# A recurrent time-mix and expert kernel: the first step spread over eight PSUM banks and reordered, weights loaded in five groups, and the waits at the start of steps three and seventeen rewritten

## The chip, the cores and the metric

One core of one Trainium2 chip runs the whole program. The metric is the device time of the program in microseconds (us), the median over several executions; lower is better. Before the change it is 1033.22 us (3 runs, 1031.26 to 1033.80).

## What is computed

The input x is (2, 2048, 256), two sequences of 2048 tokens with 256 channels, all in fp32. It is layer-normed, and two branches share the result:

```
xn = layernorm(x)
s = timemix(xn)            # six mixed inputs r,w,k,v,a,g; low-rank tanh products; k normed;
                           # wkv7 recurrence over the tokens, 4 heads of 64; group norm; + bonus; * g; @ oW
g = silu(ffn(xn))          # 8 experts, top 2 of softmax(gate), relu(x wi + bi + lora_e), @ wo
out = x + s * g
```

Inside `timemix`: `dx = x_last - x`, `xm = x + dx*x_miu`, `mix = tanh(xm x_A)`, `miu = lambdas + mix x_B`, and each mixed input is `x + dx*miu` (`xd` in the kernel). Then `k = k_in kW + tanh(k_in k_A) k_B`, divided by its norm; `w` from `tanh(w_in w_A) w_B`; the gates from `a_in a_A a_B` and `tanh(g_in g_A) g_B`; `r` and `v` are full products.

## The kernel before

The 2048 tokens are worked through in 16 tiles of 64 tokens for each of 2 groups and both sequences (`TILES` = 16). The pipeline has three stages, "front" (everything up to r, k, v and the gates of a tile), "rec" (the chunked recurrence and the expert products of the tile before) and "post" (output product and store of the tile before that). So there are `TILES` + 2 = 18 steps; step 1 has front alone, step 2 front and rec, steps 3 to 16 all three, step 17 rec and post, step 18 post.

Each engine has its program written out by hand, one list for each kind of step; engines meet through semaphores alone. `till(name, n)` is the count that a semaphore of the tile in hand must reach. Names that matter below:

- PE (TensorE), from L242: `warm(n)` (L291) issues n products of 256 columns whose result nobody reads. Each product of fp32 stands in the trace as two matmul rows. `xt_`, `route`, `mix`, `miu(0..2)`, `wk_A`, `kW`, `wk_B`, `norm`, `a_A`, `a_B`, `r_`, `xmt_`, `g_A`, `g_B`, `v_` and `bonus_` are the front's products in the order of step 1; with `half=True` a product is split in two of 64 columns of weights that run side by side. `diag` (L439) closes a front. `base`, `lora` (L251) and `gram(l)` (L465) open the recurrence step; `gram(0)` waits in `barrier` (L593) for the end markers of the other three engines, `act_end`, `dve_end` and `pool_end`.
- VectorE: `mixed(k)` (L1393) forms (miu + lambda)*dx into `mtmp`; `first_expert`, `first_mask`, `second_expert`, `expert_masks` and `gate_sum` are chains of very small operations; `key_norm` (L1446, L1447), `kh_` (L1452), `bk0` (L1467), `dg2_` (L1459), `ar1` and `diag_store` end the front.
- GpSimd: `mixed(k)` (L1194) adds xnc to `mtmp` and gives `xd`; `ksum_`, and `bk1` (L1244).
- ScalarE: reads the PSUM banks into SBUF: `hwk` (tanh of wk_A), `kraw_` and `ksq`, `sig_`, `nrm_` (square root), `ha`, `agate_` (sigmoid, of a_B), `r_e`, `xmt_e`, `hg` (tanh of g_A), `ar0`, `gate_`, `v_e`. A change of function can put an `ACT_TABLE_LOAD` in front.
- SP issues the loads. The weights are in four groups, each with one semaphore that counts all its members; PE waits for group 1 before `miu(0)` (L342).

Order and waits in step 1 come from the PSUM banks. `USED_BY` gives every front product bank 3 or 4, the two banks of `miu` too, since in all later steps the recurrence holds the other six. So in step 1 a product waits until the product before it in that bank has been read: `miu(2)` (banks 3 and 4) stands behind `ha_done` and `nrm_done`, `g_A` behind `r_done`, `v_` behind `bonus_done`.

How PE starts a step, L608:

```
full = 4 <= step <= TILES
if step == 2:
    pe.wait_ge(*till("v_done", 0))
    pe.wait_ge(*till("gate_done", 0))
elif not full:
    barrier(step)
```

## Time and profile before

| | us |
|---|---|
| median of 3 runs | 1033.22 |
| the profiled execution | 1030.45 |
| its span (first to last instruction) | 1028.6 |
| step 1: first `gram(0)` of step 2 begins | 47.00 |
| from there to `gram(0)` of step 3 | 62.22 |
| from there to `gram(0)` of step 4 | 62.21 |
| most later steps | 61.35 |

The span is what the trace covers; the profiled execution's own time is 1.85 us longer. In the rows further down, a timeline row reads: start in us, duration in us, engine, line, operation, output and inputs, count, and in brackets how long the engine was idle before and what ended that. PE is the matmul, PEld the weight load. Line numbers are those of the kernel before; in the changed kernel they are 1 to 3 higher.

### The profile page before, as it was taken

How to read it: one execution, taken by the hardware profiler on the slowest of the kernel's cores; microseconds unless marked ns; L12 is line 12 of the kernel's file. 1: busy time of each engine (PE TensorE's matmuls, PEld its weight loads, DVE VectorE, ACT ScalarE, POOL GpSimd, SP SyncE). 2: the span in 40 equal slices, each digit the busy share in tenths (PEclk: the TensorE clock that was granted, in tenths of full speed). 3: DMA queues.
4: the chain of work that ended last, by engine and by line, in shares of the span. 5: the costliest groups of instructions: out<-in, count | busy, mean ns of one | idle time of the engine just before them, and what ended most of it. 6: DMA issues, size and time to landing. Idle time of an engine off the chain costs nothing.

```text
span 1028.6 us, 45507 instructions
## 1 busy us (share of the span) xinstructions
PE 1004.7 (98%) x19960; PEld 787.4 (77%) x19960; DVE 840.2 (82%) x1674; ACT 664.0 (65%) x1460; POOL 457.6 (44%) x541
## 2 busy tenths in 40 slices
PE   8899999999999999999999999999999999999996
PEld 5677777777787777878778787777878778787774
DVE  4597878888898898888888898888889889798764
ACT  3457575766766577675766767577685666757453
POOL 3353353635436353453625436354443725445322
PEclk9999999999999999999999999999999999999998
DMA  7000000000000000000000000000000000000000
GB/s 248 2 13 3 2 4 23 3 23 3 4 23 4 22 3 3 22 4 23 4 23 3 3 23 4 22 4 4 21 4 24 3 23 3 3 22 4 12 4 21
DMA packets 9267, 17.13 MB, mean 17 GB/s; under 512 B 1904, under 2 KB 3824, under 8 KB 8816
## 3 DMA queue, kind: packets, MB, share of 16 engines
q1 hardware_dynamic: 9072, 14.23, 4.3%
q8 instruction: 159, 2.61, 1.1%
q14 instruction: 36, 0.29, 0.1%
HBM read 10.03 MB, written 4.19 MB: 14 GB/s over the span
## 4 chain that ended last, share of the span: by engine, by line
PE 89%; DVE 5%; issue 2%; ACT 2%; SPq 1%; DMA 0%; POOLq 0%; POOL 0%; DVEq 0%
PE bank L251 36%; PE bank L250 13%; PE grams L465 10%; PE bank L342 5%; PE grams L534 2%; PE bank L491 2%; PE bank L480 2%; PE bank L524 2%; PE bank L565 2%; PE grams L589 2%; PE grams L554 2%; PE grams L439 2%; PE bank L357 2%; PE bank L373 2%; PE bank L299 2%
## 5 line engine op out<-in xcount | busy, mean ns | idle before, releaser
L1213 POOL TENSOR_TENSOR bk<-bk,tot 128x256 f32<-128x256 f32 x192 | 154.7, 817 | 214.6 <-PE grams L465 214.6
L1527 DVE COPY_PREDICATED gm<-c_mask_g,grams 128x1024 f32<-128x1024 int32 x96 | 160.2, 1669 | 15.1 <-PE grams L465 14.4
L899 ACT ACTIVATE relu<-bank,prm 128x256 f32<-128x256 f32 x256 | 107.3, 471 | 88.0 <-PE bank L251 86.7
L1194 POOL TENSOR_TENSOR xd<-mtmp,xnc 128x512 f32<-128x512 f32 x96 | 120.9, 1274 | 35.9 <-DVE mtmp L1393 35.9
L251 PE MATMUL bank<-xnc,w_wi 128*128 128x256 f32 x512 | 125.5, 388 | 3.8 <-ACT scratch L1181 2.1
L465 PEld LDWEIGHTS grams<-ar,bk 64*64 64x64 f32 x6144 | 100.9, 135 | 23.2 <-issue 15.4
L1003 ACT ACTIVATE gl<-gm 32x128 f32<-32x128 f32 x320 | 98.9, 309 | 28.6 <-DVE gm L1527 21.9
L251 PE MATMUL bank<-xmt,w_lora_B 128*128 128x256 f32 x444 | 114.5, 387 | 0.0
L465 PE MATMUL grams<-ar,bk 64*64 64x64 f32 x6144 | 112.0, 221 | 2.4 <-ACT scratch L1181 2.3
L251 PEld LDWEIGHTS bank<-xnc,w_wi 128*128 128x128 f32 x512 | 95.0, 191 | 22.2 <-issue 6.9
L1537 DVE TENSOR_TENSOR ar<-ar,tot 128x512 f32<-128x512 f32 x96 | 93.1, 970 | 20.9 <-PE grams L465 20.9
L1393 DVE SCALAR_TENSOR_TENSOR mtmp<-bank,prm,dx 128x256 f32<-128x256 f32 x192 | 80.3, 473 | 29.0 <-PE bank L342 29.0
L1244 POOL TENSOR_TENSOR bk<-kh,rootd 128x512 f32<-128x512 f32 x16 | 28.2, 1763 | 151.9 <-PE bank L524 150.3
L251 PEld LDWEIGHTS bank<-xmt,w_lora_B 128*128 128x128 f32 x444 | 80.5, 190 | 15.1 <-issue 5.0
L250 PE MATMUL bank<-w_wo,hid 128*64 128x256 f32 x768 | 90.9, 379 | 0.0
L250 PEld LDWEIGHTS bank<-w_wo,hid 128*64 128x64 f32 x768 | 52.6, 137 | 23.3
L342 PE MATMUL bank<-mixt,w_x_B 32*128 32x256 f32 x384 | 54.4, 400 | 1.1 <-DMA c_headsel<-c_headsel_dram 0.9
L1225 POOL TENSOR_TENSOR out_t<-out_t,x_in 128x512 f32<-128x512 f32 x16 | 20.3, 1270 | 76.7 <-DVE out_t L1516 76.7
L1495 DVE TENSOR_TENSOR hid<-relu 128x512 f32<-128x512 f32 x64 | 48.3, 775 | 0.6
L910 ACT ACTIVATE xnc<-bank 128x512 f32<-128x512 f32 x16 | 9.6, 598 | 50.8 <-PE bank L299 50.8
L945 ACT ACT_TABLE_LOAD x32 | 41.1, 1283 | 0.6
L1576 DVE TENSOR_TENSOR state<-dec,bank 128x256 f32<-128x256 f32 x32 | 13.4, 418 | 33.2 <-PE bank L575 33.2
(189 smaller groups left out, 2232.6 us busy)
## 6 DMA issues: line engine op xcount, KB each, us to landing
x_in<-x SPq DMA_DIRECT2D x16, 256.0 KB, 2.7
out<-out_t SPq DMA_DIRECT2D x16, 256.0 KB, 2.0
w_wi<-w_wi_dram SPq DMA_DIRECT2D x1, 1024.0 KB, 6.3
w_wo<-w_wo_dram SPq DMA_DIRECT2D x1, 1024.0 KB, 8.6
w_lora_B<-w_lora_B_dram SPq DMA_DIRECT2D x1, 512.0 KB, 7.3
w_x_A<-w_x_A_dram SPq DMA_DIRECT2D x1, 256.0 KB, 2.7
w_x_B<-w_x_B_dram SPq DMA_DIRECT2D x1, 256.0 KB, 2.8
w_kW<-w_kW_dram SPq DMA_DIRECT2D x1, 256.0 KB, 3.3
```

The lines of the kernel that those rows point to most:

```text
L250: last = mm(out[o:o + 64, :], lhsT[:, o:o + 64], rhs, **kw)
L251: return last if half else mm(out, lhsT, rhs, **kw)
L342: last = mm(MIU[k % 2][:, c * 256:(c + 1) * 256], w["x_B"][o:o + 32, u, c * 128:(c + 1) * 128], mixt[o:o + 32, u, :], start=True, stop=True)
L465: last = mm(dst, bk[o:o + 64, g, c, 1 - b, k, :], rhs, start=True, stop=True)
L899: A(dst[:, p % 2, j * 256:(j + 1) * 256], ZB[p % 2][:, j * 256:(j + 1) * 256], ACT.Relu, bias=prm[:, P_BI + 2 * p + j:P_BI + 2 * p + j + 1 ...
L1003: A(gl[l % 2][o:o + 32, :, :, :].rearrange("p q g (c n m) -> p (q g c) n m", c=2, m=m), right(gm[o:o + 32, :, :, :, b, 0, 32 * k:32 * k + ...
L1194: tt(xd[:, q, :, :], mtmp[:, k % 2, :, :], xnc[steps["front"] % 2][:, :, :], ALU.add).then_inc(S(f"xd_{k}_done"), 1)
L1213: tt(v, v, d, ALU.mult).then_inc(S(f"bk{k}_scaled"), 1)
L1393: run(v.scalar_tensor_tensor(mtmp[:, k % 2, c, :], MIU[k % 2][:, c * 256:(c + 1) * 256], prm[:, P_LAM + 2 * q + c:P_LAM + 2 * q + c + 1], ...
L1495: run(v.tensor_tensor(hid[:, p, :], relu1[:, p % 2, :], relu2[:, p % 2, :], ALU.add), f"hid_{p}_done")
L1527: run(v.copy_predicated(dst, msk.to_broadcast([128, 32, HALF // m, m]), src), "g_stored")
L1537: run(v.tensor_tensor(a, a, tv[:, :, 0].unsqueeze(1).unsqueeze(3).to_broadcast([128, 2, 4 * n, m]), ALU.mult), "ar_scaled")
```

## The change

In step 1 a table of its own, `FIRST_USED_BY`, spreads the front's products over banks 0 to 6, and `warm` writes bank 7 in place of 2. With it go a new order on PE, ScalarE, VectorE and GpSimd in step 1, other numbers of `warm` products, and a weight group more. At the start of steps the waits of PE are rewritten. The diff, cut to its core:

```diff
+FIRST_USED_BY = {"xt": 0, "route": 2, "mix": 1, "kW": 5, "wk_A": 6, "g_A": 0, "wk_B": 2, "a_A": 1, "a_B": 5, "norm":
+           6, "r": 0, "v": 2, "g_B": 1, "xmt": 5, "bonus": 6}
...
-            return bank[USED_BY[name]]
+            return bank[(FIRST_USED_BY if steps["front"] == 0 else USED_BY)[name]]
...
-        SECOND = ["x_B", "w_A", "k_A", "a_A", "wk_B", "a_B", "kW", "rW", "vW", "g_A", "g_B", "ones", "headsel"]
+        SECOND = ["x_B", "w_A", "k_A", "wk_B", "kW"]
-        THIRD = ["wi", "lora_B"]
+        THIRD = ["ones", "a_A", "a_B", "g_A", "rW", "vW", "g_B", "headsel"]
+        FOURTH = ["wi", "lora_B"]
...
-                    mm(CB[:, 0:256], xnc[1][:, 0, 0:128], xnc[1][:, 1, :], start=True, stop=True)
+                    mm(FB[:, 0:256], xnc[1][:, 0, 0:128], xnc[1][:, 1, :], start=True, stop=True)
...
-                full = 4 <= step <= TILES
+                full = 3 <= step <= TILES
                 if step == 2:
-                    pe.wait_ge(*till("v_done", 0))
-                    pe.wait_ge(*till("gate_done", 0))
-                elif not full:
+                    pe.wait_ge(*till("mx_4_done", 0))
+                    pe.wait_ge(*till("mx_5_done", 0))
+                    pe.wait_ge(*till("xmt_done", 0))
+                    pe.wait_ge(*till("bonus_done", 0))
+                elif step == TILES + 2:
                     barrier(step)
                 if step == 1:
-                    warm(6)
+                    warm(5)
...
+                        warm(4)
                         if step == 1:
                             wait_loaded(pe, 1)
                         miu(0)
-                        warm(3)
+                        warm(4)
...
                         miu(1)
+                        kW(half=True)
+                        wk_A()
+                        wait_loaded(pe, 2)
+                        g_A(half=True)
+                        wk_B()
+                        a_A()
+                        miu(2)
+                        a_B()
+                        norm()
+                        warm(2)
+                        r_()
+                        v_()
+                        g_B()
                         xmt_()
+                        warm(3)
+                        bonus_()
                         pe.wait_ge(*till("r_done", 1))
+                        pe.wait_ge(*till("gate_done", 1))
                         diag(rec)
...
                         hwk()
+                        hg()
                         kraw_()
+                        ha()
                         sig_()
+                        agate_()
                         nrm_()
-                        ha()
-                        agate_()
                         r_e()
+                        gate_(step)
+                        ar0(rec)
                         xmt_e()
-                        hg()
-                        ar0(rec)
-                        gate_(step)
                         v_e(rec)
...
                         mixed(1)
                         mixed(0)
+                        mixed(3)
+                        mixed(2)
                         ksum_()
-                        mixed(2)
-                        mixed(3)
...
-                        first_mask()
-                        second_expert()
                         mixed(1)
                         mixed(0)
                         mixed(3)
                         mixed(2)
+                        gate_sum()
+                        first_mask()
+                        second_expert()
                         expert_masks()
                         mixed(4)
+                        mixed(5)
                         decay_step(rec)
-                        mixed(5)
                         key_norm()
                         kh_()
+                        dg2_()
                         bk0(rec)
-                        dg2_()
+                        ar1(rec)
                         bonus_e(rec)
-                        gate_sum()
-                        ar1(rec)
...
                         top_x()
+                        pe.wait_ge(*till("v_done", 0))
                         keys_to_tokens(0)
...
                         rec_p(1)
+                        pe.wait_ge(*till("gate_done", 0))
                         keys_to_tokens(1)
```

The last two pieces are step 17's; in step 17's own list `barrier(step)` still stands as the first entry, ahead of `gram(0)`, in both kernels. `full` also puts the waits for `v_done` before `xt_` and for `gate_done` before `route` in step 3.

PE in the middle of step 1, before: `a_A` (a_A), `miu(2)` (x_B), `a_B`, `r_` (rW), with `warm` products (xnc) between.

```order
L363 MATMUL bank<-xd,w_a_A 64x256 [waits xd_2_done,sig_done]
L363 MATMUL bank<-xd,w_a_A 64x256
L294 MATMUL bank<-xnc 128x256 x4
L342 MATMUL bank<-mixt,w_x_B 128x256 [waits mixt_done,ha_done,nrm_done]
L342 MATMUL bank<-mixt,w_x_B 128x256 x3
L294 MATMUL bank<-xnc 128x256 x2
L251 MATMUL bank<-h_a,w_a_B 128x256 [waits ha_done,mx_4_done]
L251 MATMUL bank<-h_a,w_a_B 128x256
L251 MATMUL bank<-xd,w_rW 128x256 [waits xd_4_done,mx_5_done]
L251 MATMUL bank<-xd,w_rW 128x256 x3
```

The same place in the changed kernel, from `a_A` on:

```order
L366 MATMUL grams<-xd,w_a_A 64x256 [waits xd_2_done,mixt_done]
L366 MATMUL grams<-xd,w_a_A 64x256
L345 MATMUL bank<-mixt,w_x_B 128x256 [waits mixt_done,mx_3_done,mx_2_done]
L345 MATMUL bank<-mixt,w_x_B 128x256 x3
L254 MATMUL bank<-h_a,w_a_B 128x256 [waits ha_done,ksq_done,kraw_done]
L254 MATMUL bank<-h_a,w_a_B 128x256
L254 MATMUL bank<-ksum,c_ones 128x256 [waits ksum_done,hwk_done]
L297 MATMUL bank<-xnc 128x256 x2
L254 MATMUL grams<-xd,w_rW 128x256 [waits xd_4_done,hg_done]
L254 MATMUL grams<-xd,w_rW 128x256 x3
```

`miu(2)` follows `a_A` directly and no longer waits for `ha_done` and `nrm_done`; `norm` (ksum) has moved behind `a_B`.

PE at the end of step 1, before: `bonus_` (dg), `g_B`, `v_` (vW), `diag` (rr), and the first product of step 2 (wi).

```order
L446 MATMUL bank<-dg,c_headsel 32x128 [waits dg2_done,xmt_done]
L446 MATMUL bank<-dg,c_headsel 32x128 x3
L251 MATMUL bank<-w_g_B,h_g 128x256 [waits hg_done]
L251 MATMUL bank<-w_g_B,h_g 128x256
L251 MATMUL bank<-w_vW,xd 128x256 [waits xd_5_done,bonus_done]
L251 MATMUL bank<-w_vW,xd 128x256 x3
L439 MATMUL grams<-rr,bk 64x64 [waits r_done,bk1_ready,bk0_ready]
L439 MATMUL grams<-rr,bk 64x64 x31
L251 MATMUL bank<-xnc,w_wi 128x256 [waits v_done,gate_done,big_buffers_zeroed,xnc_done,weights_loaded_3,weights_loaded_2]
```

The same place in the changed kernel; the `warm` products stand ahead of `bonus_`:

```order
L297 MATMUL bank<-xnc 128x256 x3
L449 MATMUL bank<-dg,c_headsel 32x128 [waits dg2_done,nrm_done]
L449 MATMUL bank<-dg,c_headsel 32x128 x3
L442 MATMUL grams<-rr,bk 64x64 [waits bk1_ready,bk0_ready,r_done,gate_done]
L442 MATMUL grams<-rr,bk 64x64 x31
L254 MATMUL bank<-xnc,w_wi 128x256 [waits mx_5_done,mx_4_done,xmt_done,big_buffers_zeroed,bonus_done,weights_loaded_4,xnc_done,weights_loaded_3,weights_loaded_2]
```

`g_B` and `v_` have gone from between `bonus_` and `diag`, and step 2 no longer waits for `v_done`.

PE at the start of step 3, before: `v_`, `base(1)` (wi), `lora(1)`, `gram(0)`.

```order
L251 MATMUL bank<-w_vW,xd 128x256 [waits xd_5_done,bonus_done]
L251 MATMUL bank<-w_vW,xd 128x256 x3
L251 MATMUL bank<-xnc,w_wi 128x256 [waits xnc_done,dve_end,relu2_3_done,pool_end,act_end]
L251 MATMUL bank<-xnc,w_wi 128x256 x3
L251 MATMUL bank<-xmt,w_lora_B 128x256 [waits xmt_done]
L251 MATMUL bank<-xmt,w_lora_B 128x256
L465 MATMUL grams<-ar,bk 64x64 [waits dve_end,pool_end,act_end]
```

The same place in the changed kernel:

```order
L254 MATMUL bank<-w_vW,xd 128x256 [waits xd_5_done,bonus_done]
L254 MATMUL bank<-w_vW,xd 128x256 x3
L254 MATMUL bank<-xnc,w_wi 128x256 [waits relu2_3_done,xnc_done]
L254 MATMUL bank<-xnc,w_wi 128x256 x3
L254 MATMUL bank<-xmt,w_lora_B 128x256 [waits xmt_done]
L254 MATMUL bank<-xmt,w_lora_B 128x256
L468 MATMUL grams<-ar,bk 64x64 [waits dve_end,pool_end,act_end]
```

The three end markers have gone from `base(1)` and stand ahead of `gram(0)` alone.

## Rows read from the trace of the kernel before

**Rows 1.** The page: busy time by engine, the chain that ended last.

```profile
PE 1004.7 (98%) x19960; PEld 787.4 (77%) x19960; DVE 840.2 (82%) x1674; ACT 664.0 (65%) x1460; POOL 457.6 (44%) x541
...
PE 89%; DVE 5%; issue 2%; ACT 2%; SPq 1%; DMA 0%; POOLq 0%; POOL 0%; DVEq 0%
```

**Rows 2.** Stretches of step 1 (us; PE, PEld, DVE, ACT, POOL busy; PEclk; DMA share; GB/s).

```profile
37.28:40.70 3.42, 3.42 (x15) 2.52 (x13) 1.59 (x6) 0.60 (x1) 0.00 (x0) 0.50 0.00 0
33.87:37.28 3.41, 1.52 (x12) 0.86 (x13) 2.60 (x4) 1.86 (x4) 1.87 (x2) 1.00 0.01 2
```

**Rows 3.** DMA issues (KB, us to landing), then start, us, engine of SP and PE.

```profile
w_kW<-w_kW_dram SPq DMA_DIRECT2D x1, 256.0 KB, 3.3
...
7.35 0.43 SPq L1799 DMA_DIRECT2D w_kW<-w_kW_dram  x1
...
11.89 0.59 PE L294 MATMUL bank<-xnc 128*128 128x256 f32 x2
13.36 1.13 PE L342 MATMUL bank<-mixt,w_x_B 32*128 32x256 f32 x8 [0.87 <-DMA c_headsel<-c_headsel_dram]
```

**Rows 4.** Timeline of step 1, first half: DVE, GpSimd and PE.

```profile
14.54 1.66 DVE L1393 SCALAR_TENSOR_TENSOR mtmp<-bank,prm,dx 128x256 f32<-128x256 f32 x4 [2.10 <-PE bank L342]
...
15.49 2.49 POOL L1194 TENSOR_TENSOR xd<-mtmp,xnc 128x512 f32<-128x512 f32 x2 [11.08 <-DVE mtmp L1393]
...
16.25 1.13 PE L342 MATMUL bank<-mixt,w_x_B 32*128 32x256 f32 x8 [0.27 <-DVE mtmp L1393]
```

**Rows 5.** Timeline of ScalarE, 22 to 32 us.

```profile
23.37 1.28 ACT L945 ACT_TABLE_LOAD   x1
...
26.82 0.38 ACT L977 ACTIVATE nrm<-bank 128x256 f32<-128x256 f32 x1
...
27.62 0.38 ACT L931 ACTIVATE h_a<-bank 128x256 f32<-128x256 f32 x1
```

**Rows 6.** Timeline of VectorE and GpSimd, 29 to 38 us, and one line's durations.

```profile
29.26 0.88 DVE L1393 SCALAR_TENSOR_TENSOR mtmp<-bank,prm,dx 128x256 f32<-128x256 f32 x2 [9.29 <-PE bank L342]
...
31.17 0.58 DVE L1446 TENSOR_SCALAR nrm<-nrm 128x256 f32<-128x256 f32 x1
...
33.64 0.69 DVE L1452 TENSOR_TENSOR kh<-kraw,kinv 128x512 f32<-128x512 f32 x1
...
36.15 0.87 DVE L1459 SCALAR_TENSOR_TENSOR dg<-rr,prm,kh 128x256 f32<-128x256 f32 x2
...
34.41 1.27 POOL L1244 TENSOR_TENSOR bk<-kh,rootd 128x512 f32<-128x512 f32 x1 [1.54 <-DVE kh L1452]
...
L1467 DVE SCALAR_TENSOR_TENSOR bk<-kh,agate x16: 691/692/1347, 34.9 to 955.8; 128x512 f32<-128x512 f32 x16
```

**Rows 7.** Timeline of PE, end of step 1 and start of step 2.

```profile
39.56 2.46 PE L251 MATMUL bank<-w_vW,xd 128*128 128x256 f32 x8
41.95 1.16 PE L439 MATMUL grams<-rr,bk 64*64 64x64 f32 x64
44.24 1.97 PE L251 MATMUL bank<-xnc,w_wi 128*128 128x256 f32 x8 [1.14 <-ACT vt L973]
...
47.00 1.17 PE L465 MATMUL grams<-ar,bk 64*64 64x64 f32 x64
```

**Rows 8.** The same at step 2 to 3, with ScalarE's end marker.

```profile
102.46 1.89 PE L251 MATMUL bank<-w_vW,xd 128*128 128x256 f32 x8
106.46 1.97 PE L251 MATMUL bank<-xnc,w_wi 128*128 128x256 f32 x8 [2.11 <-ACT scratch L1181]
...
109.22 1.17 PE L465 MATMUL grams<-ar,bk 64*64 64x64 f32 x64
```

**Rows 9.** The same at step 3 to 4, and at step 16 to 17.

```profile
167.02 1.89 PE L251 MATMUL bank<-w_vW,xd 128*128 128x256 f32 x8
...
171.43 1.17 PE L465 MATMUL grams<-ar,bk 64*64 64x64 f32 x64
...
968.91 1.85 PE L465 MATMUL grams<-ar,bk 64*64 64x64 f32 x64 [2.32 <-ACT scratch L1181]
```

More of the change, by code:

```diff
@@ L96, in program @@
         x_first = ctx.enter_context(nc.semaphore("first_x_loaded"))
-        loaded_by = [ctx.enter_context(nc.semaphore(f"weights_loaded_{i}")) for i in range(4)]
+        loaded_by = [ctx.enter_context(nc.semaphore(f"weights_loaded_{i}")) for i in range(5)]
         zeroed = ctx.enter_context(nc.semaphore("buffers_zeroed"))
@@ L628, in tile @@
                         miu(1)
-                        warm(1)
-                        pe.wait_ge(*till("mx_3_done", 2))
-                        wk_A()
-                        pe.wait_ge(*till("mx_2_done", 2))
-                        kW(half=True)
-                        pe.wait_ge(*till("hwk_done", 1))
-                        wk_B()
-                        warm(4)
+                        kW(half=True)
+                        wk_A()
+                        wait_loaded(pe, 2)
+                        pe.wait_ge(*till("xnc_done", 1))
@@ L637, in tile @@
+                        g_A(half=True)
+                        pe.wait_ge(*till("route_read", 1))
+                        wk_B()
+                        pe.wait_ge(*till("mixt_done", 2))
+                        a_A()
+                        pe.wait_ge(*till("mx_2_done", 2))
+                        pe.wait_ge(*till("mx_3_done", 2))
+                        miu(2)
                         pe.wait_ge(*till("kraw_done", 1))
                         pe.wait_ge(*till("ksq_done", 1))
-                        norm(half=True)
@@ L640, in tile @@
-                        warm(1)
+                        a_B()
+                        pe.wait_ge(*till("hwk_done", 1))
+                        norm()
+                        warm(2)
+                        pe.wait_ge(*till("hg_done", 1))
+                        r_()
                         pe.wait_ge(*till("sig_done", 2))
-                        a_A()
-                        warm(4)
-                        pe.wait_ge(*till("nrm_done", 1))
+                        v_()
                         pe.wait_ge(*till("ha_done", 1))
-                        miu(2)
@@ L647, in tile @@
-                        warm(2)
-                        pe.wait_ge(*till("mx_4_done", 2))
-                        a_B()
-                        pe.wait_ge(*till("mx_5_done", 2))
-                        r_()
+                        g_B()
                         pe.wait_ge(*till("agate_done", 2))
                         xmt_()
+                        warm(3)
+                        pe.wait_ge(*till("nrm_done", 1))
+                        bonus_()
                         pe.wait_ge(*till("r_done", 1))
-                        g_A()
@@ L656, in tile @@
-                        pe.wait_ge(*till("xmt_done", 1))
-                        bonus_()
-                        pe.wait_ge(*till("hg_done", 1))
-                        g_B()
-                        pe.wait_ge(*till("bonus_done", 1))
-                        v_()
+                        pe.wait_ge(*till("gate_done", 1))
                         diag(rec)
@@ L881, in tile @@
                     wait_loaded(pe, 3)
+                    wait_loaded(pe, 4)
                     pe.wait_ge(zeroed_late, len(ZEROED_LATE))
@@ L1774, in tile @@
                         if step == 1:
[L1775 removed]
+                            wait_loaded(dve, 4)
                             dve.wait_ge(zeroed_late, len(ZEROED_LATE))
@@ L1809, in _ @@
                     load(3)
+                    load(4)
                 if step >= 3:
```

17 lines of the change are left out of this document (5 added, 12 removed).

## Prediction

> **What bounds the kernel now.** I read the page first. PE is busy for 98% of the span and carries 89% of the chain that ended last [rows 1], so in general only PE's own work and the places where PE has nothing to do are worth anything. The change leaves the steady steps alone: PE's order in steps 2 to 18 is the same, only waits differ. So I looked at two places: step 1, where there is no recurrence to fill PE, and the seams between steps. The stretches of step 1 show what is left there: from 33.87 to 37.28 us PE is busy for 1.52 of 3.41 us, and in the next 3.42 us it is busy throughout but at a granted clock of 0.50, that is 1.2 GHz [rows 2]. Then the timelines of each engine, in the order in which the wait ends last: loads, VectorE, ScalarE, VectorE again, PE.
>
> **Step 1, up to miu(0).** Before, miu(0) is released at 13.36 us by headsel, the thirteenth load of its group [rows 3]. The group of five ends with w_kW, which even at its old place (issued at 7.35, 3.3 us to landing) is there at 10.65 us [rows 3]. So that wait is gone. But three more warm products stand in its place. The warm products after mix begin at 11.89 us [rows 3]. Ten products of this shape (v_, base, lora) take 167.02 to 171.43, 0.44 us each [rows 9], so four last until 13.65 us. miu(0) begins 0.3 us **later** than before: the new group gains nothing here. miu(1) follows 2.89 us behind it [rows 3, 4], the four warm products between (1.76 us, after 1.1 us of miu) fit in just that, and mtmp and xd on VectorE and GpSimd keep their distance [rows 4]. miu(1) is at 16.55 us, and GpSimd's first two xd end at 18.3.
>
> **Up to ksq.** PE now does kW, wk_A and g_A where it did one warm product, wk_A and kW. By 0.44 a product that is some 0.9 for g_A less 0.44 and less a wait for mtmp: wk_B comes about 0.2 us later than before, and so do kraw and ksq, whose end before is the table load at 23.37 [rows 5]. Now 23.6 us.
>
> **ScalarE to nrm.** Before, 23.37 to 26.82 holds a table load (1.28), the sigmoids, and another load: 3.45 us, so 0.89 for a pair of sigmoids [rows 5]. The new order adds h_a (0.38 alone, some 0.3 in a row of reads) before and the pair of agate within: 23.6 + 0.3 + 3.45 + 0.85 = 28.2, and nrm (0.38) ends at 28.55, which is 1.35 us later than its 27.20 of before [rows 5]. That agate's product is there in time rests on miu(2) and a_B: miu(2) starts at about 22.9, a_B follows h_a at about 24, agate is not due until 26.
>
> The Trainium skill, page ScalarE: Activation LUTs, section What ACT_TABLE_LOAD costs, puts a switch at about 1.28 us of load and 1.38 us of drain, 2.66 in all. By that the two switches of this chain would cost 2.8 us more, and the time would be 1025.0. The trace has 1.28 and nothing beside it at these two.
>
> **VectorE to kh.** Here is the first gain. Before, VectorE sat idle for 9.29 us until 29.26 because miu(2) stood behind ha_done and nrm_done, and key_norm began only at 31.17 although nrm was there at 27.20 [rows 5, 6]. Now miu(2) is done at 24.0, mixed(4) and mixed(5) (0.88 each [rows 6]) fit before 26.5, and key_norm begins with nrm at 28.6. From key_norm to the end of kh is 31.17 to 34.33, 3.16 us [rows 6], of which some 0.1 or 0.2 was the first operation being held up. kh ends at 31.6: **2.73 us earlier**.
>
> What hides the rest: the chains of small operations (first_mask and so on) now run between mixed(2) and mixed(4), 19.5 to about 24.5; each 1 us more pushes r_ back by 1. The PE chain r_ (from 26.7), v_, g_B, xmt, warm(3) is about 14 products or 6.2 us and ends at 32.9, 0.9 ahead of its due time. If that cover is gone, every us over it counts.
>
> **kh to diag.** Before: bk0, dg2, then bonus, g_B and v_ on PE, the last two at the half clock (v_ takes 2.46 against 1.89 [rows 7, 8]), then diag at 41.95: 7.62 us after kh [rows 6, 7]. Now g_B and v_ lie ahead, and dg2 (0.87) and bk0 remain. GpSimd's bk1 starts with the same signal and takes 1.27 [rows 6]. bk0 took 1.35 beside it and 0.69 in the median [rows 6], so a VectorE operation is held while GpSimd runs. Between "not held" (0.87 + 0.69, diag at 33.3) and "held to the end of bk1" (1.27 + 0.87 + 0.69, diag at 34.5) I take the second, because the row of step 1 is the very case. That is 2.9 us after kh in place of 7.62: **4.72 us earlier**.
>
> **diag to gram(0) of step 2.** Before 5.05 us, with 1.14 of waiting for the last copy of v [rows 7]. Now base(1) waits for xmt_done and bonus_done instead. bonus_e ends at about 35.4, diag's 1.1 us of issue at 35.6, so they just fit. Then 44.24 to 47.00, 2.76 us [rows 7]: gram(0) comes 3.85 us behind diag, at 38.35. **1.20 us earlier**. The end markers don't hold it: diag_store (1.3 us) ends 2.6 us behind diag, the copies of v on ScalarE at about 35.2. If ScalarE were 2.8 us later than that, it would be the end.
>
> Together 2.73 + 4.72 + 1.20 = **8.65 us**. The order of functions on ScalarE also ends step 1 with the square root, and the load ahead of step 2's std goes; base(0) and lora(0) cover that time on PE, so nothing is counted (0 to 0.3).
>
> **Step 3.** Before, PE idles 2.11 us for act_end, then base(1); v_ to gram(0) is 102.46 to 109.22, 6.76 us [rows 8]. At the next seam, where base and lora already stand ahead of the wait, it is 4.41 [rows 9]. Difference **2.35 us**. The idle time of before ended with act_end at 106.46 [rows 8], so a gram(0) at 102.46 + 4.41 = 106.87 is not early for it. The added waits for v_done and gate_done come after gram(0), which has waited for act_end, and cost nothing.
>
> **Step 17.** The barrier is taken from the head of the step, but the step's own list still begins with it ahead of gram(0), so the idle 2.32 us [rows 9] stay: 0. If it worked as the words of the change say, PE could have saved those 2.3 (1019.9); the order of the changed kernel excludes that.
>
> **Sum.** 8.65 + 2.35 = 11.0 us. Against the profiled execution 1030.45 - 11.0 = 1019.45; the median of the runs lies 2.77 above that execution, so 1033.22 - 11.0 = **1022.2**.
>
> **Rivals.**
> - *VectorE isn't held by bk1.* 1.2 us more, 1021.0. For it: dg2 could start before GpSimd takes its turn. Chance 0.12.
> - *The clock falls at the end of step 1.* Before it fell after 33.87 to 37.28, with PE busy for 1.52 us [rows 2]. Now PE is thin from 33 to 34.5 alone. A stretch of 3.4 us at 1.2 GHz costs up to 1.7: 1023.9. Chance 0.12.
> - *The barrier at step 3 only changes places*: gram(0) is held by the markers. Then 2.35 is lost, 1024.55. Against it stands the seam behind it. Chance 0.04.
> - *The table switch has its drain* in the new order: 1025.0. Chance 0.04.
> - *Slower: the clock is never granted in step 1.* One warm product fewer stands at the start, and PE has a gap ahead of xt_. The new step 1 has some 52 products of 0.44, 23 us; at 1.2 GHz that is some 20 more, of which 4 fall into gaps: 1022.2 + 16 = 1038. It decides from 11 us of such work on. Before, the granted clock was 1.00 from 33.87 to 37.28 [rows 2], with a start that differs by one product of six, so 0.01. The Trainium skill, page TensorE: Matmul & The Clock Gate, section What's actually happening, says that the default is throttled and activity releases it; by that rule too one product fewer matters little.
>
> **How the numbers follow.** The forecast has 0.62, the rivals 0.33, and 0.05 is left for what I don't see. The range: a gain of 8.5 us (clock and some small delays, 1024.7) to 13 (not held, the saved table load, fewer stalls of issue, which are 2% of the chain [rows 1]; 1020.2), and 0.5 to 1 for the scatter of the median, whose three runs lie 2.5 apart: 1019.2 to 1025.2. About 0.3% (3.1 us) is what a measurement of this kernel can tell from no change. Faster by more 0.96, within it 0.02, slower 0.02.
>
> **What would show it.** Right: miu(0) at about 13.6, not earlier; miu(2) at 23 and VectorE's long idle gone; kh at 31 to 32; diag within 3 us of kh; PEclk 1.00 up to 969 us; gram(0) of step 2 at 38, of step 3 some 59.9 later; the seam at step 17 unchanged. Wrong: PE idle ahead of bonus_ or diag for over 1.5 us, VectorE's small operations running past 25, PEclk at 0.50 after 30, or a start of step 3 still behind ACT scratch.

## The result, and the profile after

The changed kernel takes **1017.13 us** (median of 4 runs, 1016.44 to 1018.04) against 1032.24 us for the kernel before beside it (4 runs, 1030.65 to 1033.80): a ratio of 0.9862, with a 95% interval of 0.9842 to 0.9881. Two later sets gave 0.9869 [0.9846, 0.9892] and 0.9867 [0.9852, 0.9882]. These four runs of the kernel before lie high: the medians differ by 15.1 us here, by 13.5 and 13.6 in the later sets, which have 13 runs of it each. I take 13.7 us as the gain; the narrowest of the intervals allows 12.2 to 15.2. The forecast was 1022.2, in a range from 1019.2 to 1025.2. The direction was right, the time lies below the range.

| | before | after |
|---|---|---|
| the profiled execution, us | 1030.45 | 1017.24 |
| its span | 1028.6 | 1015.4 |
| `gram(0)` of step 2 begins | 47.00 | 38.25 |
| from there to `gram(0)` of step 3 | 62.22 | 59.56 |
| `gram(0)` of step 17 begins | 968.91 | 956.80 |

The page of the changed kernel, beside [rows 1]. PE's busy time is 6.8 us less, with eight matmul rows fewer: the kernel hardly computes less, it waits less and computes less slowly.

```profile
span 1015.4 us, 45487 instructions
...
PE 997.9 (98%) x19952; PEld 783.6 (77%) x19952; DVE 842.5 (83%) x1674; ACT 660.5 (65%) x1458; POOL 457.3 (45%) x541
...
PE 93%; DVE 3%; issue 2%; ACT 2%; POOLq 0%; POOL 0%; DVEq 0%
```

**Step 1.** PE's timeline in the changed kernel, which answers to [rows 3, 4, 7]:

```profile
12.01 1.89 PE L297 MATMUL bank<-xnc 128*128 128x256 f32 x8
13.83 1.13 PE L345 MATMUL bank<-mixt,w_x_B 32*128 32x256 f32 x8
...
23.09 1.13 PE L345 MATMUL bank<-mixt,w_x_B 32*128 32x256 f32 x8
...
33.68 0.43 PE L449 MATMUL bank<-dg,c_headsel 128*32 128x128 f32 x8 [0.30 <-DVE dg L1460]
34.34 1.16 PE L442 MATMUL grams<-rr,bk 64*64 64x64 f32 x64 [0.24 <-issue]
35.49 1.97 PE L254 MATMUL bank<-xnc,w_wi 128*128 128x256 f32 x8
...
38.25 1.17 PE L468 MATMUL grams<-ar,bk 64*64 64x64 f32 x64
```

`miu(0)` begins with the end of the warm products, not with a load. `miu(2)` is at 23.09, where before it was held until 28.09 by the reads of two banks. `diag` is at 34.34 in place of 41.95, and behind it there is no wait any more.

VectorE in the same stretch, beside [rows 6], and then ScalarE, beside [rows 5]:

```profile
24.73 1.65 DVE L1394 SCALAR_TENSOR_TENSOR mtmp<-bank,prm,dx 128x256 f32<-128x256 f32 x4
...
28.61 0.29 DVE L1447 TENSOR_SCALAR nrm<-nrm 128x256 f32<-128x256 f32 x1 [1.39 <-ACT nrm L978]
28.94 1.75 DVE L1448 RECIPROCAL kinv<-nrm 128x256 f32<-128x256 f32 x1
30.81 0.69 DVE L1453 TENSOR_TENSOR kh<-kraw,kinv 128x512 f32<-128x512 f32 x1
31.61 1.92 DVE L1460 SCALAR_TENSOR_TENSOR dg<-rr,prm,kh 128x256 f32<-128x256 f32 x2
33.45 0.68 DVE L1468 SCALAR_TENSOR_TENSOR bk<-kh,agate 128x512 f32<-128x512 f32 x1
```

```profile
24.03 1.28 ACT L946 ACT_TABLE_LOAD   x1
25.32 0.84 ACT L946 ACTIVATE sig<-bank,prm 128x256 f32<-128x256 f32 x2
26.05 0.84 ACT L946 ACTIVATE agate<-bank,prm 128x256 f32<-128x256 f32 x2
26.90 1.28 ACT L978 ACT_TABLE_LOAD   x1
28.20 0.38 ACT L978 ACTIVATE nrm<-bank 128x256 f32<-128x256 f32 x1
```

The idle time of 9.29 us on VectorE is gone, and the longest wait left in this stretch is 1.39 us for nrm. The pair of dg takes 1.92 us beside GpSimd's bk1.

**The seams.** Step 2 to 3, where the wait of 2.11 us of [rows 8] is gone:

```profile
93.40 1.89 PE L254 MATMUL bank<-w_vW,xd 128*128 128x256 f32 x8
95.13 1.89 PE L254 MATMUL bank<-xnc,w_wi 128*128 128x256 f32 x8
96.86 1.03 PE L254 MATMUL bank<-xmt,w_lora_B 128*128 128x256 f32 x4
97.81 1.17 PE L468 MATMUL grams<-ar,bk 64*64 64x64 f32 x64
```

and step 16 to 17, where most of it stayed, beside [rows 9]:

```profile
956.80 1.17 PE L468 MATMUL grams<-ar,bk 64*64 64x64 f32 x64 [2.01 <-ACT scratch L1182]
```

What differs here is less the wait (2.01 for 2.32) than the matmuls: 1.17 us for 64 of them, against 1.85 in the kernel before. Its own stretches tell why (columns: PE, PEld, DVE, ACT, POOL busy; PEclk; DMA share; GB/s; kernel before):

```profile
965.70:969.12 3.42, 1.10 (x18) 0.68 (x20) 2.68 (x6) 2.08 (x5) 0.19 (x1) 1.00 0.10 37
969.12:972.53 3.41, 3.41 (x68) 2.97 (x62) 1.72 (x1) 0.00 (x0) 1.67 (x3) 0.50 0.00 0
```

and the same place and the end of step 1 in the changed kernel, there with PE alone:

```profile
33.86:37.28 3.42, 3.18 (x80) 1.00 0.03 5
...
950.00:953.40 3.40, 3.40 (x85) 1.00 0.02 5
953.40:957.00 3.60, 1.59 (x19) 1.00 0.20 73
```

Before, PE ran at 1.2 GHz for 3.4 us behind the seam at step 17, with work in all of it. After, the granted clock stays 1.00 there and at the end of step 1 ([rows 2] have 0.50 from 37.28 on).

**Where 13.2 us between the two profiled spans lie**, read as distances on PE between `mix`, `miu(0)`, `diag` and `gram(0)` of the two timelines:

| stretch | before | after | gain |
|---|---|---|---|
| start to `mix` | 10.11 | 10.28 | -0.17 |
| `mix` to `miu(0)`, step 1 | 3.25 | 3.55 | -0.30 |
| `miu(0)` to `diag`, step 1 | 28.59 | 20.51 | 8.08 |
| `diag` to `gram(0)` of step 2 | 5.06 | 3.91 | 1.15 |
| `gram(0)` to `diag`, step 2 | 53.40 | 53.09 | 0.31 |
| `diag` to `gram(0)` of step 3 | 8.82 | 6.47 | 2.35 |
| `gram(0)` to `diag`, step 3 | 55.74 | 55.43 | 0.31 |
| `diag` to `gram(0)` of step 17 | 6.27 | 5.96 | 0.31 |
| `gram(0)` of step 17 to the end | 59.70 | 58.60 | 1.10 |

Together 13.1; the steps between them give the other 0.1. The row "`gram(0)` to `diag`, step 3" is no part of the change: over all profiled executions, with and without the change, it lies between 54.8 and 56.5, by stalls of issue that come and go.

Two of these rows hide something that only further executions show. From `miu(0)` to `diag` the old step 1 takes 26.94 or 26.95 us in each of the five profiled executions that have it with the granted clock at 1.00 (two of them with more warm products), and the new one 20.51 or 20.52 in eight. So the change itself is worth 6.44 us there, and the other 1.64 of the 8.08 is the stretch at 1.2 GHz of the first profiled execution. And `miu(0)` of before waits for a load, which in that execution landed early. In the kernel before, profiled again (c_before_a), the same row reads:

```profile
13.90 1.13 PE L342 MATMUL bank<-mixt,w_x_B 32*128 32x256 f32 x8 [1.84 <-DMA c_headsel<-c_headsel_dram]
```

From `mix` to `miu(0)` it is 3.25, 4.22, 3.69, 4.05 and 4.08 us in the five executions with the loads and the one warm product of before, 3.86 in the mean, and 3.55 in every one with the new loads and four warm products.

### The profile page after: what moved, and what is told of

It reads as the page before. It is cut to its first block, busy times and chain, and to the rows that moved or that the text cites. A ratio compares the mean times of both kernels' runs of the same rounds, so it can differ in the third digit from the quotient of the medians.

```text
span 1015.4 us, 45487 instructions
## 1 busy us (share of the span) xinstructions
PE 997.9 (98%) x19952; PEld 783.6 (77%) x19952; DVE 842.5 (83%) x1674; ACT 660.5 (65%) x1458; POOL 457.3 (45%) x541
## 4 chain that ended last, share of the span: by engine, by line
PE 93%; DVE 3%; issue 2%; ACT 2%; POOLq 0%; POOL 0%; DVEq 0%
PE bank L254 37%; PE bank L253 14%; PE grams L468 10%; PE bank L345 5%; PE bank L494 2%; PE grams L537 2%; PE bank L483 2%; PE bank L527 2%; PE grams L442 2%; PE bank L568 2%; PE grams L592 2%; PE grams L557 2%; PE bank L360 2%; PE bank L376 2%; PE bank L302 2%
## 5 line engine op out<-in xcount | busy, mean ns | idle before, releaser
L254 PEld LDWEIGHTS bank<-xmt,w_lora_B 128*128 128x128 f32 x444 | 80.5, 190 | 15.1 <-issue 5.0
L1203 POOL TENSOR_TENSOR tot<-tot 128x256 f32<-128x256 f32 (+2 forms) x96 | 39.5, 412 | 2.7
```

What stands on the lines that cost most here:

```text
L254: return last if half else mm(out, lhsT, rhs, **kw)
```

## The experiments

**The halves.** First the two kernels unchanged, beside everything else.

c_before_a (the kernel before): 

> The kernel before, unchanged, for its own scatter. Theory A (the runs of before that lie above its fastest are executions in which the clock fell at a seam where PE had nothing to do): times from 1030 to 1034, and the slower ones have the lower mean granted clock, about 0.990 at 1033.5 against 0.993 at 1030.5. Rival B (the scatter has nothing to do with the clock): the same spread with the same mean clock in all.

Measured 1030.98 (10 runs, 1029.21 to 1033.76), ratio 1.0001 [0.9988, 1.0015]. In step 1 its profiled execution had the slow stretch at another place than the first: a granted clock of 0.50 from 15.48 on for 6.8 us, where the first had it at 37.28; at step 17 both had one. The slower runs have the lower clock, as theory A has it: 0.990 in the one of 1033.76 us, 0.995 in the one of 1029.21.

c_after (the changed kernel): 

> The changed kernel, unchanged, beside the kernel before on the same chip. Theory A (part of the gain is clock falls that no longer come): about 14 us less than the median of before (1031), that is 1017, with a spread of about 1.5 and a mean granted clock of 0.995 or more. Rival B (my prediction's way of counting, the gap between median and profiled execution stays the same in both kernels): the same 11 us less, 1020.

Measured 1017.22 (4 runs, 1015.71 to 1017.81), ratio 0.9869.

e_first_only: step 1 and step 2 as changed, the waits of steps 3 and 17 as before.

```diff
-                full = 3 <= step <= TILES
+                full = 4 <= step <= TILES
...
-                elif step == TILES + 2:
+                elif not full:
                     barrier(step)
```

> The changed kernel with the old starts of steps 3 and 17 (barrier at their head). The first step's part alone. By the traces: gram(0) of step 2 at 38.25 in place of 47.00 (8.75) and 0.3 in step 2 (no table load ahead of std): about 9.0 us less than before. Theory A: 1023 with the same scatter of about 3 as before, since the idle seam 2 to 3 is still there. Rival B: 1023 as well; rival C (the two parts help each other beyond their sum): over 1024.

Measured 1022.01 (4 runs), ratio 0.9913 [0.9886, 0.9939]: 9.0 us of the gain. A and B said the same here, so it decides only against C.

e_seams_only: the kernel before, with the changed waits of steps 3 and 17 alone.

```diff
-                full = 4 <= step <= TILES
+                full = 3 <= step <= TILES
...
-                elif not full:
+                elif step == TILES + 2:
                     barrier(step)
...
+                        pe.wait_ge(*till("v_done", 0))
                         keys_to_tokens(0)
...
+                        pe.wait_ge(*till("gate_done", 0))
                         keys_to_tokens(1)
```

> The kernel before with the new starts of steps 3 and 17 alone. By the traces 2.35 us at step 3; at step 17 the same three markers are waited for once in place of twice, which my prediction priced at nothing and the trace of the changed kernel shows as 0.3 us (2.01 idle in place of 2.32). Theory A: 2.65 and another 1 to 1.5 of clock falls that no longer come at step 3: about 1028.4. Rival B: 2.65 alone, 1029.6; rival D (the 0.3 at step 17 is chance): idle 2.3 at step 17, 1029.9.

Measured 1027.46 (9 runs), ratio 0.9969 [0.9957, 0.9981]: 3.2 us. The timelines give the seams 2.35 + 0.31 = 2.66, with 6.47 and 5.96 us from `diag` to `gram(0)`, as in the changed kernel. That rules out rival D; A (3.65 to 4.15) and B (2.65) both lie within the interval of 2.0 to 4.4 us. The halves add up to 12.2 of 13.7, within the intervals. In e_first_only the seams' idle time is still there, and PE's timeline shows what it costs beside itself:

```profile
96.87 2.82 PE L254 MATMUL bank<-xnc,w_wi 128*128 128x256 f32 x8 [2.12 <-ACT scratch L1182]
99.48 1.90 PE L254 MATMUL bank<-xmt,w_lora_B 128*128 128x256 f32 x4
101.32 1.17 PE L468 MATMUL grams<-ar,bk 64*64 64x64 f32 x64
```

The eight rows take 2.82 us, where the changed kernel has 1.89, and the four 1.90 in place of 1.03. The seam is 10.52 us long in this execution: 8.82 and 1.7 more of slow clock.

**The terms of the sum, one by one.**

e_warm1: one warm product ahead of `miu(0)` in place of four.

```diff
                         mix()
-                        warm(4)
+                        warm(1)
```

> The changed kernel with one warm product in place of four ahead of miu(0), the number that the kernel before has there. Theory (miu(0) stands behind these products and nothing else, mixt being there at 12.85): miu(0) at 12.9 in place of 13.83, everything up to diag 0.9 earlier, 1016.2. Rival (the chain to diag starts later than miu(0), or the products hold the clock up): diag at 34.3 as now or later, 1017 or more, with a fall of the clock in the record.

PE's timeline of e_warm1:

```profile
11.46 0.59 PE L297 MATMUL bank<-xnc 128*128 128x256 f32 x2
12.45 1.13 PE L345 MATMUL bank<-mixt,w_x_B 32*128 32x256 f32 x8 [0.39 <-ACT mixt L920]
```

`miu(0)` stands 1.0 us behind the warm product's start in place of 1.82, and `mix` to `diag` is 23.23 in place of 24.07: 0.84 us, all of which the chain passes on. The median is 1016.65 (4 runs), ratio 0.9866. That is less than 0.84 below the changed kernel, and the two intervals overlap, so the traces show this gain and the medians don't resolve it. What `miu(0)` waits for now is ScalarE's second piece of mixt, by 0.39 us.

e_group: the changed kernel with the weight groups of before. 

```diff
-        SECOND = ["x_B", "w_A", "k_A", "wk_B", "kW"]
+        SECOND = ["x_B", "w_A", "k_A", "a_A", "wk_B", "a_B", "kW", "rW", "vW", "g_A", "g_B", "ones", "headsel"]
...
-                        wait_loaded(pe, 2)
                         pe.wait_ge(*till("xnc_done", 1))
```

> The changed kernel with the weights in the four groups of before (headsel thirteenth in the second group). Theory A (the new group gains nothing, since miu(0) stands behind the four warm products): miu(0) at 13.6 to 13.9 and gram(0) of step 2 at 37.8 to 38.3, as in the changed kernel. Theory B (the group matters): miu(0) later than 14.2 and everything behind it by as much.

```profile
11.79 1.89 PE L297 MATMUL bank<-xnc 128*128 128x256 f32 x8
13.85 1.13 PE L345 MATMUL bank<-mixt,w_x_B 32*128 32x256 f32 x8 [0.17 <-DMA c_headsel<-c_headsel_dram]
```

`miu(0)` at 13.85 against 13.83, but `mix` began earlier here: from `mix` to `miu(0)` it is 3.78 for 3.55, and `mix` to `diag` is 24.30, 0.2 more. The one run took 1018.20 us. In this execution the load ends just behind the warm products, and the fifth group is worth 0.2 us. In the seven executions with the old loads and the old step 1, `miu(0)` was released between 13.36 and 14.13, and in most executions of the changed kernel the warm products are done by 13.4, so elsewhere the group should be worth up to some 0.7 us, an estimate from these rows. It is also what e_warm1 needs, with `miu(0)` at 12.45.

e_bk1_dve: GpSimd's bk1 of step 1 moved to VectorE, behind bk0.

```diff
                         bk0(rec)
+                        bk1_v()
...
-                        bk1(rec)
```

> The changed kernel with bk1 of step 1 on VectorE, behind bk0, instead of on GpSimd. Theory A (dg2 of VectorE was held by GpSimd's bk1 for 1.05 us): dg2 takes 0.87 each, bk0 ends 1.0 earlier, bk1 then costs 0.7 to 0.9 on VectorE but diag needs only dg2 and bk0, or bk1 too: diag 0.2 to 1.0 us earlier, mix to diag 23.1 to 23.9 against 24.07. Theory B (dg2 was slow for a reason of its own): dg2 stays at 1.92 and diag comes 0.7 to 0.9 us later.

VectorE's timeline of e_bk1_dve:

```profile
31.17 0.88 DVE L1459 SCALAR_TENSOR_TENSOR dg<-rr,prm,kh 128x256 f32<-128x256 f32 x2
31.97 0.68 DVE L1467 SCALAR_TENSOR_TENSOR bk<-kh,agate 128x512 f32<-128x512 f32 x1
32.57 0.68 DVE L1474 TENSOR_TENSOR bk<-kh,rootd 128x512 f32<-128x512 f32 x1
```

The pair of dg takes 0.88 when GpSimd is idle and 1.92 when it is not: the hold is real, and it was GpSimd's. `mix` to `diag` is 23.66, 0.41 less, since bk1 now takes 0.6 of VectorE's own time. The median, 1017.65 (4 runs), shows nothing of it; the profiled execution lost more at step 17, where its clock fell.

e_vwait: the two waits of before put back at the head of step 2.

```diff
                     pe.wait_ge(*till("bonus_done", 0))
+                    pe.wait_ge(*till("v_done", 0))
+                    pe.wait_ge(*till("gate_done", 0))
```

> The changed kernel with the two waits of before (v_done, gate_done) put back at the head of step 2, beside the new ones. Theory A (v is read out of its bank before diag's last product is issued): diag to gram(0) 3.9 to 4.2 us. Theory B (the move of the two waits is what the seam gains): 4.4 us or more.

`diag` to `gram(0)` is 4.01 for 3.91, and the one run took 1016.29. All other executions with the new step 1 have 3.91. So the seam of step 2 gained by v being early, not by the waits being other ones; two waits that are already met cost 0.10.

e_sqrt_end: the kernel before with a square root in ScalarE's order behind `ar0`, so that step 1 ends with that table.

```diff
                         ar0(rec)
+                        A(scratch[:, 0:1], eps[:, 0:1], ACT.Sqrt)
                         gate_(step)
```

> The kernel before with one square root of a scratch column on ScalarE near the end of step 1, where ScalarE is idle, so that step 2 finds the table of the square root in place. Theory: this is the whole of the 0.3 us that step 2 is shorter in the changed kernel: from gram(0) of step 2 to that of step 3 61.9 in place of 62.22 (clock falls aside), gram(0) of step 2 where it was. Rival: 62.2 as before, and the 0.3 comes from VectorE's later start in step 2. The median 0.3 less, which the timing can't tell; the trace decides.

ScalarE's load ahead of rstd in step 2 (47.97 in the kernel before) is gone, and `gram(0)` to `diag` of step 2 is 53.11 in place of 53.40, just the 53.09 of the changed kernel. The load lay on the path with at most 0.3 of its 1.28 us: e_fill, e_fill2 and e_fill3 below keep it and have 53.26, 53.25 and 53.26, with nothing changed in step 2, so half of the difference may be something else. The median is 1030.85, ratio 1.0004 [0.9990, 1.0018]: too small for it.

e_base17: step 17 as its description has it, with `base(1)` and `lora(1)` ahead of the barrier.

```diff
+                        base(1)
+                        lora(1)
                         barrier(step)
                         gram(0)
-                        base(1)
-                        lora(1)
```

> The changed kernel with what the words of the change say of step 17: base(1) and lora(1) ahead of the barrier, then gram(0) and gram(1). The rival of my prediction prices this at 2.0 us less (the idle time of PE). Other theory: step 17 hangs on VectorE's chain gram(0), store, scale, gram(1), so what counts is when gram(0) begins; base and lora end 0.6 us after the markers, so gram(0) is 0.6 later and the time 0.6 more, though PE's idle time at the seam is gone.

Measured 1018.31 (4 runs), ratio 0.9881 [0.9863, 0.9898], not faster than the changed kernel. PE has work until `gram(0)`, but that now begins 4.41 us behind `v_`, where the changed kernel has 3.90, and the chain on VectorE behind it comes later by as much, with less of PE's work left to cover it:

```profile
956.47 1.17 PE L468 MATMUL grams<-ar,bk 64*64 64x64 f32 x64
957.70 2.47 DVE L1528 COPY_PREDICATED gm<-c_mask_g,grams 128x1024 f32<-128x1024 int32 x1 [1.67 <-PE grams L468]
959.99 0.87 DVE L1538 TENSOR_TENSOR ar<-ar,tot 128x512 f32<-128x512 f32 x1
960.91 1.39 PE L468 MATMUL grams<-ar,bk 64*64 64x64 f32 x44 [3.28 <-DVE ar L1538]
```

PE idles 3.28 us for `ar` instead of 2.01 for the marker and 0.50 for `ar`, and its stretches show the clock that follows:

```profile
957.60:961.04 3.44, 0.16 (x11) 0.13 (x11) 3.16 (x2) 0.79 (x3) 3.19 (x5) 1.00 0.00 0
961.04:964.45 3.41, 3.41 (x68) 3.02 (x69) 1.56 (x2) 0.45 (x2) 2.18 (x5) 0.50 0.02 5
```

So the forecast was right that the change does not do this, and wrong that it would have saved 2.3 us: `gram(0)` begins 0.5 us later behind `v_`, and the time is no shorter.

**What the terms leave over.** The timelines' terms without slow clock are worth about 10.9 us (worked out in the next section), the measured gain is some 13.7, so 2.8 are left, 1.3 to 4.3 by the interval. Theory A: the rest is time at 1.2 GHz that the kernel before pays behind its idle seams. Rival B: waits that the timelines don't show.

e_fill: the kernel before, with products that nobody reads in the idle time of the seams; nothing is taken away.

```diff
                 elif not full:
+                    if step in (3, TILES + 1):
+                        warm(4)
                     barrier(step)
```

> The kernel before with four warm products ahead of the barrier in steps 3 and 17, so that PE is busy for 1.7 of its 2.1 to 2.3 idle us there. No work is taken out. Theory A: the granted clock no longer falls after these two seams; the median goes down by 1 to 2 us to about 1030.5 and its spread to under 2; in the profile the interval from v_ to gram(0) of step 3 stays at 6.76. Rival B: median and spread as before, 1032.2 and 3.

Measured 1029.11 (10 runs), ratio 0.9987 [0.9971, 1.0003]. In its profiled execution the granted clock falls behind neither seam, as A has it, but its runs spread over 4.0 us where A said under 2, and the interval reaches 1: leaning to A, open.

e_fill2: meant as e_fill with more products in step 1, but its four products of steps 3 and 17 stand behind the barrier, so the idle time is not filled as the expectation has it.

```diff
                     barrier(step)
...
+                if step in (3, TILES + 1):
+                    warm(4)
```

> The kernel before with more work and none taken away: four warm products at the head of steps 3 and 17, one more ahead of miu(0), three ahead of bonus_ and two behind diag in step 1, all where PE idles. Theory A (the part of the gain that the timelines don't explain, 2.8 us, is time at 1.2 GHz that the kernel before pays in most executions and the changed one does not): granted clock 1.00 up to the tail, median 1027.5 to 1029, and a scatter no wider than that of the changed kernel (2 us). Theory B (the 2.8 us lie in waits inside step 1 and the seams): median within 1 us of the kernel before, some 1031, or later by the products added.

Measured 1034.44 (12 runs), ratio 1.0021 [1.0007, 1.0035]. It tests nothing of A: the products lie on the path, and the idle time stays. But PE's timeline shows the price of a slow stretch on the very same work:

```profile
104.95 3.42 PE L294 MATMUL bank<-xnc 128*128 128x256 f32 x8 [2.05 <-ACT scratch L1185]
```

3.42 us for eight rows that take 1.89 otherwise; `diag` to `gram(0)` of step 3 is 12.17 us.

e_fill3: the same kernel with the products ahead of the barrier.

```diff
                 elif not full:
+                    if step in (3, TILES + 1):
+                        warm(4)
                     barrier(step)
...
                         mix()
-                        warm(1)
+                        warm(2)
...
+                        warm(3)
                         pe.wait_ge(*till("xmt_done", 1))
                         bonus_()
...
                         diag(rec)
+                        warm(2)
```

> As the run with products at the heads of steps 3 and 17, but there they stand ahead of the barrier, where PE idles, and not behind it: the kernel before, with four warm products ahead of the barriers of steps 3 and 17, one more ahead of miu(0), three ahead of bonus_ and two behind diag in step 1. Theory A (the rest of the gain, 2.8 us, is time at 1.2 GHz): diag to gram(0) of step 3 at 8.8 and of step 17 at 6.3 as before, granted clock 1.00 up to the tail, median 1027.5 to 1029. Theory B (the rest lies in waits inside step 1 and the seams): median 1030 to 1032, as the kernel before.

Beside it c_after_b, the changed kernel: 

> The changed kernel unchanged, beside the filled kernel of before. Theory A: it lies 10.5 to 11.5 us below the filled one (the structural terms alone), and 13.5 to 14 below the kernel before. Theory B: the distance to the filled kernel is 13.5 to 14 too.

e_fill3 takes 1028.17 (9 runs), ratio 0.9983 [0.9971, 0.9994], and c_after_b 1016.87 (4 runs), ratio 0.9867 [0.9852, 0.9882]. PE's timeline of e_fill3 at step 3:

```profile
102.59 1.89 PE L294 MATMUL bank<-xnc 128*128 128x256 f32 x8
104.97 1.97 PE L251 MATMUL bank<-xnc,w_wi 128*128 128x256 f32 x8 [0.49 <-ACT scratch L1185]
...
107.73 1.17 PE L465 MATMUL grams<-ar,bk 64*64 64x64 f32 x64
```

No wait and no transfer is gone, 28 matmul rows are added, and the kernel is faster than before by 2.3 us (1.7 by the ratio). From the filled kernel to the changed one it is 11.3 us by the medians and 11.9 by the two ratios, where A said 10.5 to 11.5 and B 13.5 to 14. So added work alone gives back **about 2 us of the 2.8** (1.7 to 2.3; the interval of the ratio allows 0.6 to 3.0), and B, which said 1030 to 1032, is out for these.

How much of it is the clock can be told a second way. A stretch at a granted 0.50 costs PE at most half of its length, so the difference of the mean granted clocks, times the length of the run, is an upper limit. For e_fill3 that is 0.9954 against 0.9942 beside it, at most 1.2 us. For the changed kernel it is 0.9956 (12 runs) against 0.9934 (77), at most 2.3 us of the 2.8. At least 0.5 us of the rest is therefore not slow clock; it lies within the intervals and stays open.

e_best: the changed kernel with `warm(1)` ahead of `miu(0)`, bk1 on VectorE, and products in the idle time of the last two seams and ahead of the last `o_`. `fill` is `warm` with bank 5 for its result.

```diff
+                elif step == TILES + 1:
+                    fill(4)
                 elif step == TILES + 2:
+                    fill(6)
                     barrier(step)
...
+                        if not rec:
+                            fill(2)
                         o_(half=True)
```

> The changed kernel with one warm product instead of four ahead of miu(0), bk1 of step 1 on VectorE, four filling products at the head of step 17, six ahead of the barrier of the last step and two ahead of its o_. Theory A (clock and waits as I read them): mix to diag 22.5 to 23.3, granted clock 1.00 to the end, o_ 1.9 us instead of 3.7: 2.5 to 3.5 us less than the changed kernel, median 1013.7 to 1014.7. Theory B (the clock of the tail doesn't follow PE's own work): o_ stays at 3.7 and the median is 1015.7 to 1016.7.

Measured **1013.42** (4 runs, 1013.06 to 1013.67), ratio 0.9822 [0.9806, 0.9839]: 3.5 to 3.8 us below the three medians of the changed kernel (4.1 to 4.8 by the ratios), and the best of all. It is a little faster than A's 1013.7 to 1014.7, with 22.82 us from `mix` to `diag` as A had it, and B is out. The mean granted clock of its profiled execution is 1.000. The last `o_` in the changed kernel and then here:

```profile
1007.23 3.68 PE L253 MATMUL bank<-w_oW,zt 128*64 128x256 f32 x16 [1.36 <-ACT zt L988]
```

```profile
999.30 2.86 PE L301 MATMUL bank<-xnc 128*128 128x256 f32 x12
...
1003.37 1.03 PE L301 MATMUL bank<-xnc 128*128 128x256 f32 x4
1005.36 1.95 PE L253 MATMUL bank<-w_oW,zt 128*64 128x256 f32 x16 [0.95 <-ACT zt L997]
```

1.73 us of it. Its four runs lie within 0.6 us, the 17 of before beside it within 6.0.

## Why the prediction was wrong in size, step by step

- *miu(0) 0.3 us later, at about 13.65*: 13.83 with a `mix` 0.17 later, so right against the execution that it was read from. But there the load landed earlier behind `mix` than in any other execution of the old step 1 with one warm product, and against their mean `miu(0)` comes 0.3 us **earlier** behind `mix` (3.55 for 3.86). "The new group gains nothing here" does not hold: 0.2 us in e_group, and e_warm1 rests on it.
- *ksq until 23.6, nrm until 28.55, kh until 31.6*: 23.73, 28.58 and 31.50. Right. The table load took 1.28 us with nothing beside it; the rival with a drain is out.
- *PE's products ahead of bonus_ end 0.9 us before they are due*: they ended at 33.38 and `bonus_` began at 33.68. The cover held, with 0.3 us.
- *VectorE held by bk1, diag at 34.5*: 34.34. The hold is shown by e_bk1_dve; it is 1.04 us (1.92 less 0.88), where the forecast had all 1.27 of bk1. *3.85 us from diag to gram(0)*: 3.91. Step 1 in all 8.65: **8.75**. But 1.6 us of that was the slow clock of the one execution that the forecast read (28.59 us from `miu(0)` to `diag` where it is 26.95 at full clock). It is no part of what the change does to the waits.
- *The table load of step 2 at nothing (0 to 0.3)*: 0.31 between the two profiled executions, its upper end; by e_sqrt_end and the three filled kernels 0.15 to 0.3.
- *Step 3, 2.35*: 2.35, and 4.41 us from `v_` to `gram(0)` as forecast.
- *Step 17 at 0*: **0.31**. The wait stayed, but before PE waited for the same three markers twice, at the head of the step and in `gram(0)`; the second time they were long met. e_seams_only has the 0.31 too. Two waits that are met cost 0.10 in e_vwait.
- *The clock falls at the end of step 1 after the change*: it did not; in the ten profiled executions with the new step 1 the granted clock is 1.00 from its start to its end.

Without slow clock that is 0.3 (`mix` to `miu(0)`, in the mean) + 6.44 (`miu(0)` to `diag`) + 1.15 + 0.31 + 2.35 + 0.31 = 10.9 us, and the forecast had 11.0. That the two are so near is in part luck: the forecast's 11.0 has 1.6 us of slow clock in it, and lacks 0.6 for the load and 0.6 for the two terms put at nothing.

What failed is the last step, **"the median of the runs lies 2.77 above that execution, so 1033.22 - 11.0 = 1022.2"**. It took 2.77 us as a fixed offset between a profiled execution and a median, and so as a part of the changed kernel too. The changed kernel has none: 1017.24 profiled, 1017.13 median. With it went the assumption that the profiled execution shows all that the seams of before cost:

- *Scatter of three runs.* The 77 executions of the kernel before that were timed later have a median of 1030.78 (1027.81 to 1034.72), 2.4 us below the three that the forecast stood on and 0.3 above the profiled one.
- *Slow clock as a cost of the idle time.* Of those 77, the 11 with a mean granted clock of 0.996 took 1029.31 on average, the 16 with 0.991 took 1032.69. The correlation is -0.80. The changed kernel has 1015.71 to 1018.04 in 12 executions, at 0.9956 in the mean against 0.9934. The stretches in the traces say where: in five profiled executions with the seam of before at step 17, the clock fell behind it in four; in eight with the changed waits, in one (e_bk1_dve); in three with a filled seam, in none. At step 3 it fell in three of five with the idle seam and in none of the others. In step 1 it fell in two of the five with the old step 1 unfilled, and in none of ten with the new one. Each such stretch of 3.4 us cost between 1.1 us (step 17) and 1.7 us (step 3), 1.6 in step 1; the one of 6.8 us in step 1 of c_before_a cost 2.5 (29.42 us from `miu(0)` to `diag`, for 26.95).

At step 17 the change leaves 2.01 us of idle time in place of 2.32, and yet the falls went from four in five to one in eight. These are few executions, and why 0.3 us less should do that, no run shows.

The forecast looked at the clock as a danger for the changed kernel alone, at the end of step 1, and let it stand at 969 us in the kernel before, because the wait there was to stay. It should have priced the loss behind every idle seam that the change touches, as a part of the gain: at step 3 the profiled execution showed none, and it was there in others. Of the miss of 5.1 us, 2.4 are the three runs, 0.6 the two small terms priced at nothing, 0.1 step 1 and 1.1 the slow stretch behind step 17 that did not come back; some 0.4 are stalls of issue that differ from run to run, and the last 0.4 is how far the medians lie from the profiled executions. The range failed for the same reason: its gain of up to 13 us was taken from 1033.22.

What rests on the timelines alone: no run gives the new step 1 its old banks back, or its old order on one engine, so the 6.44 us are not split by experiment between the banks, the order on PE and those on the other engines.

## What to carry to other kernels

Make the sum against the profiled execution, and take the median's distance from it as scatter until several executions show that it isn't; the granted clock of each run says where the scatter comes from. Measure a wait for a load in several executions too: here its end moved by 0.8 us. Idle time on TensorE cost twice in this kernel, once itself and once, in some executions, in the work behind it at 1.2 GHz (1.1 to 1.7 us a time). A wait removed can then return more than its length, and where it can't be removed, products that nobody reads, ahead of the wait and into a free bank, bought back part of it (some 2 us in e_fill3). They must stand ahead of the wait: behind it four of them cost 1.9 us of their own, and 3.4 where the clock was at 0.50 (e_fill2).

## What was not expected of the hardware

- The lower clock is a matter of chance in the same program: over 77 executions of the kernel before, the mean granted clock went from 0.989 to 0.998. The idle seam at step 3 (2.1 us) was followed by 0.50 in three of five profiled executions and by 1.00 in two, and the price of a fall was 1.53 us on eight rows (3.42 against 1.89).
- Semaphore waits that are long met were not free on TensorE's queue: 0.10 us for two (e_vwait), and 0.31 for the second of two barriers of three waits each (step 17, e_seams_only).
- A GpSimd operation of 1.27 us beside them more than doubled a pair of VectorE operations (1.92 against 0.88). In which order the two engines take their turns, no run here tells.
